# Attention on eight cores: softmax sums moved out of step with PV, and a pair's closing transposes moved into the next pair

## The reference, cut to what matters

```
x: (4, 4096, 1024), 16 heads of 64
q, k, v = x @ Wq.T, x @ Wk.T, x @ Wv.T
attn = softmax(q k^T / 8);  out = attn v
x = layernorm(x + out)
probs = softmax(x @ router_w.T + router_b); top 6 of 16, renormalised
y = sum over experts e of gate[:, e] * (x @ expert_w[e]) (+ small eps terms)
x = layernorm(x + y)
```

## Time and profile before

| | |
|---|---|
| Median of 3 runs | 2958.87 us |
| The profiled execution | 2957.79 us |
| Its span on core 2, from the first to the last instruction | 2956.3 us |
| Spans of the 8 cores | 2940.2 to 2956.3 us |
| Mean granted TensorE clock of the cores | 0.908 to 0.910 |
| TensorE, ScalarE, VectorE busy | 80%, 38%, 24% of the span |
| The chain that ended last | PE 62%, ACT 14%, DVE 9%, issue 9%, DMA 4% |

### The profile page before, as it was taken

The page is one execution under the profiler, slowest core; times in us unless marked ns, Lnnn a source line. Parts: engine busy times, 40 slices in busy tenths (PEclk is TensorE's granted clock), DMA queues, the critical chain, the costliest instruction groups (busy, mean ns, idle before and its releaser), DMA issues.

```text
span 2956.3 us, 31850 instructions; the slowest of 8 cores (2940.2 to 2956.3 us)
## 1 busy us (share of the span) xinstructions
PE 2357.0 (80%) x11919; PEld 898.2 (30%) x12032; DVE 719.1 (24%) x1555; ACT 1121.8 (38%) x1153; POOL 59.7 (2%) x80
## 2 busy tenths in 40 slices
PE   6996988889888888888888343899995343899996
PEld 2442322222222222222222111344442111344442
DVE  2332200000000000000000444233336444233336
ACT  0000288889888888888887101000000101000000
POOL 1000100000000000000000000000000000000000
PEclk9998999999999999999999676999998676899998
DMA  6745799950000000000000200222223000221221
GB/s 88 99 73 86 93 108 113 108 65 1 1 1 1 1 1 1 1 1 1 1 1 20 74 15 7 86 86 75 69 86 124 26 15 8 86 86 60 84 86 57
DMA packets 48017, 146.90 MB, mean 50 GB/s; under 512 B 2752, under 2 KB 23264, under 8 KB 46848
## 3 DMA queue, kind: packets, MB, share of 16 engines
q0 software_dynamic: 43264, 128.09, 23.7%
q1 hardware_dynamic: 4608, 16.78, 1.6%
HBM read 197.32 MB, written 41.94 MB: 81 GB/s over the span
## 4 chain that ended last, share of the span: by engine, by line
PE 62%; ACT 14%; DVE 9%; issue 9%; DMA 4%; DVEq 1%; ACTq 0%; POOL 0%; SPq 0%; POOLq 0%
PE s_PS L644 30%; PE s_PS L295 12%; ACT s_RC L358 9%; PE s_PS L315 6%; PE s_PS L225 5%; PE s_PS L327 5%; ACT s_RC L355 4%; PE s_PS L246 4%; DVE s_RC L467 2%; DMA s_RC<-xfm 1%; PE s_PS L382 1%; DMA s_RC<-xqf 1%; DMA s_RB<-ewb 1%; DVE s_RA L658 1%; DVE s_RC L474 1%
## 5 line engine op out<-in xcount | busy, mean ns | idle before, releaser
L644 PE MATMUL s_PS<-s_RB,s_QO 128*128 128x512 bf16 x4008 | 921.5, 390 | 147.5 <-DVE s_gates L600 72.7
L295 PE MATMUL s_PS<-s_QO,s_RA 64*128 64x512 bf16 x2048 | 598.8, 397 | 103.4 <-ACT s_RC L358 62.9
L355 ACT ACTIVATE s_RC<-s_PS,s_cb 128x1024 bf16<-128x1024 f32 x512 | 570.7, 1115 | 198.0 <-PE s_PS L295 184.6
L644 PEld LDWEIGHTS s_PS<-s_RB,s_QO 128*128 128x128 bf16 x4096 | 407.2, 100 | 657.8 <-issue 208.2
L358 ACT ACTIVATE s_RC<-s_PS,s_cb 128x1024 bf16<-128x1024 f32 x512 | 567.1, 1108 | 0.3
L315 PE MATMUL s_PS<-s_RC,s_RB 128*64 128x512 bf16 x2048 | 330.3, 402 | 11.4 <-ACT s_RC L358 11.4
L702 ACT ACTIVATE s_tE<-s_tB 128x1 f32<-128x1 f32 x16 | 3.2, 203 | 881.1 <-DVE s_tB L694 881.1
L327 PE MATMUL s_PS<-s_RC,s_ozb 128*64 128x512 bf16 x2048 | 319.0, 390 | 0.0
L372 DVE CAST s_QO<-s_PS 128x1024 bf16<-128x1024 f32 x16 | 19.6, 1225 | 1190.2 <-PE s_PS L327 1190.2
L295 PEld LDWEIGHTS s_PS<-s_QO,s_RA 64*128 64x128 bf16 x2048 | 118.3, 94 | 541.7 <-issue 541.7
L661 DVE SCALAR_TENSOR_TENSOR s_RB<-s_PS,s_gates,s_RA 128x1024 f32<-128x1024 f32 x128 | 164.2, 1283 | 275.3 <-PE s_PS L644 275.3
(11 more groups left out here) (76 smaller groups left out, 634.6 us busy)
## 6 DMA issues: line engine op xcount, KB each, us to landing
s_RB<-ewb POOLq DMA_DIRECT2D x32, 2048.0 KB, 9.7
ewb<-ew POOLq DMA_DIRECT2D x16, 2048.0 KB, 171.8
s_RC<-xfm POOLq DMA_DIRECT2D x16, 1024.0 KB, 11.9
s_RC<-xtm SPq DMA_DIRECT2D x16, 512.0 KB, 3.5
y<-s_RC SPq DMA_DIRECT2D x16, 512.0 KB, 2.6
s_RC<-xqf POOLq DMA_DIRECT2D x4, 1024.0 KB, 18.3
s_RC<-wkT POOLq DMA_DIRECT2D x1, 2048.0 KB, 17.7
s_QO<-wvT POOLq DMA_DIRECT2D x1, 2048.0 KB, 27.9
```

Source lines behind the costliest of these rows:

```text
L295: ins = t.matmul(PS[:, head * 1024 + qc * 512: head * 1024 + (qc + 1) * 512], RA[rows, c * SQ + kc * 128: c * SQ + (kc + 1) * 128], QO[row ...
L355: sc.activation(P[:, 0:1024], PS[:, 0:1024], AF.Exp, bias=cb3[:, :], scale=0.125).then_inc(sE, 1)
L644: ins = t.matmul(PS[:, pb + jh * 512: pb + (jh + 1) * 512], QO[:, dc * TOK + t_i * 128: dc * TOK + (t_i + 1) * 128], wbuf(par)[:, dc * 102 ...
```

## The change

The helper `emit_pvz` becomes two, `emit_pv` and `emit_z`, which are issued separately. PV(kc-1) stays behind the scores of step kc. Z does not: steps 1 to 3 of a pair issue none, step 4 issues Z(0), Z(1) and Z(2), and each step from 5 on issues Z(kc-2), behind PV(kc-1). At the end of the pair PV(31) is followed by Z(30) and Z(31). PV(0) waits for the two large copies of the pair before, Z(0) for its small copies. The exp of step kc waits for the count behind Z(kc-4).

The transposes and the small copies of a pair are issued by `emit_ftz` in step 2 of the next pair, between its scores and PV(1). Those of the last pair stand at the end of the loops. The number of matmuls, transposes and copies is unchanged.

```
+    def emit_ftz(p_prev):
+        def ftz(t, zev=fve_cnt[p_prev]):
+            t.wait_ge(vE, zev)
+            for sl in range(8):
+                ins = t.transpose(PS[:, 3072 + sl * 128: 3072 + (sl + 1) * 128],
+                                  zs[:, sl * 128:(sl + 1) * 128], idf[:, :])
+            ins.then_inc(tV, 1)
+        q("tensor", ftz)
...   (fvz: the 16 small copies, as before)
+                if kc == 2 and p > 0:
+                    emit_ftz(p - 1)
                 if kc > 0:
                     kcp = kc - 1
-                    ve_need = cvE.v if kcp == 0 else 0
+                    ve_need = fve_cnt.get(p - 1, 0) if kcp == 0 else 0
                     def ftPV(t, c=c, kcp=kcp, exp_need=exp_need, ve_need=ve_need):
                         t.wait_ge(sE, exp_need)
                         if ve_need > 0:
                             t.wait_ge(vE, ve_need)
-                        emit_pvz(t, c, kcp, kcp == 0, False).then_inc(tV, 1)
+                        emit_pv(t, c, kcp, kcp == 0, False).then_inc(tV, 1)
+                zl = []
+                if kc == 4:
+                    zl = [0, 1, 2]
+                elif kc >= 5:
+                    zl = [kc - 2]
+                if zl:
+                    ve_need = fvz_cnt.get(p - 1, 0) if zl[0] == 0 else 0
+                    def ftZ(t, c=c, zl=tuple(zl), ve_need=ve_need):
+                        if ve_need > 0:
+                            t.wait_ge(vE, ve_need)
+                        for kcp in zl:
+                            ins = emit_z(t, c, kcp, kcp == 0, False)
+                        ins.then_inc(tV, 1)
...
-                def fse(sc, s_done=s_done, pv_need=(ctV.v - 3 if kc >= 4 else 0),
-                        kc=kc):
+                def fse(sc, s_done=s_done, kc=kc,
+                        pv_need=(z_cnt.get((p, kc - 4), 0) if kc >= 4 else 0)):
...
             def ftPVl(t, c=c, exp_need=csE.v):
                 t.wait_ge(sE, exp_need)
-                emit_pvz(t, c, NKT - 1, False, True).then_inc(tV, 1)
+                emit_pv(t, c, NKT - 1, False, True).then_inc(tV, 1)
+            def ftZl(t, c=c):
+                for kcp in (NKT - 2, NKT - 1):
+                    ins = emit_z(t, c, kcp, False, kcp == NKT - 1)
+                ins.then_inc(tV, 1)
...   (fve: the two large copies, as before; ftz and fvz at this place are gone)
+    emit_ftz(2 * NPAIR - 1)
```

More of the change, by code:

```diff
@@ L275, in build, with emit_pv, emit_z, fvz @@
     ew_cast_done = NE * 16
+    fve_cnt = {}
+    fvz_cnt = {}
+    pv_cnt = {}
+    z_cnt = {}
+    def emit_pv(t, c, kcp, first, last):
+        P = pbuf(kcp % 4)
+        for head in range(2):
+            hh = 2 * c + head
+            orow = slice(head * 64, (head + 1) * 64)
+            for qc in range(2):
+                ins = t.matmul(
+                    PS[orow, 2048 + qc * 512: 2048 + (qc + 1) * 512],
+                    RB[:, kcp * D + hh * 64: kcp * D + (hh + 1) * 64],
+                    P[:, head * 1024 + qc * 512: head * 1024 + (qc + 1) * 512],
+                    start=first, stop=last, tile_position=(0, head * 64),
+                    skip_group_check=True)
+        return ins
+    def emit_z(t, c, kcp, first, last):
+        P = pbuf(kcp % 4)
+        for head in range(2):
+            orow = slice(head * 64, (head + 1) * 64)
+            for qc in range(2):
+                ins = t.matmul(
+                    PS[orow, 3072 + qc * 512: 3072 + (qc + 1) * 512],
+                    ozb[:, :],
+                    P[:, head * 1024 + qc * 512: head * 1024 + (qc + 1) * 512],
+                    start=first, stop=last, tile_position=(0, head * 64),
+                    skip_group_check=True)
+        return ins
+    def emit_ftz(p_prev):
[6 more added lines that the diff above has]
+        q("tensor", ftz)
+        ctV.v += 1
+        ztr = ctV.v
+        def fvz(v, c=p_prev % NPAIR, h=p_prev // NPAIR, ztr=ztr):
+            v.wait_ge(tV, ztr)
+            for sl in range(8):
+                tile = h * 8 + sl
+                v.tensor_copy(rzpre[:, tile * NH + 2 * c: tile * NH + 2 * c + 1],
+                              PS[:, 3072 + sl * 128: 3072 + sl * 128 + 1])
+                ins = v.tensor_copy(
+                    rzpre[:, tile * NH + 2 * c + 1: tile * NH + 2 * c + 2],
+                    PS[:, 3072 + sl * 128 + 64: 3072 + sl * 128 + 65])
+            ins.then_inc(vE, 1)
+        q("vector", fvz)
+        cvE.v += 1
+        fvz_cnt[p_prev] = cvE.v
     for h in range(2):
@@ L344, in ftPV @@
                             t.wait_ge(vE, ve_need)
-                        emit_pvz(t, c, kcp, kcp == 0, False).then_inc(tV, 1)
+                        emit_pv(t, c, kcp, kcp == 0, False).then_inc(tV, 1)
                     q("tensor", ftPV)
                     ctV.v += 1
-                def fse(sc, s_done=s_done, pv_need=(ctV.v - 3 if kc >= 4 else 0),
-                        kc=kc):
+                    pv_cnt[(p, kcp)] = ctV.v
+                zl = []
[11 more added lines that the diff above has]
+                        ins.then_inc(tV, 1)
+                    q("tensor", ftZ)
+                    ctV.v += 1
+                    for kcp in zl:
+                        z_cnt[(p, kcp)] = ctV.v
+                def fse(sc, s_done=s_done, kc=kc,
+                        pv_need=(z_cnt.get((p, kc - 4), 0) if kc >= 4 else 0)):
                     if pv_need > 0:
@@ L364, in ftPVl, with fve @@
                 t.wait_ge(sE, exp_need)
-                emit_pvz(t, c, NKT - 1, False, True).then_inc(tV, 1)
+                emit_pv(t, c, NKT - 1, False, True).then_inc(tV, 1)
             q("tensor", ftPVl)
             ctV.v += 1
-            pv_done = ctV.v
-            def fve(v, c=c, qc0=qc0, pv_done=pv_done):
-                v.wait_ge(tV, pv_done)
+            pv_cnt[(p, NKT - 1)] = ctV.v
+            def ftZl(t, c=c):
+                for kcp in (NKT - 2, NKT - 1):
+                    ins = emit_z(t, c, kcp, False, kcp == NKT - 1)
+                ins.then_inc(tV, 1)
+            q("tensor", ftZl)
+            ctV.v += 1
+            for kcp in (NKT - 2, NKT - 1):
+                z_cnt[(p, kcp)] = ctV.v
+            pvz_done = ctV.v
+            def fve(v, c=c, qc0=qc0, pvz_done=pvz_done):
+                v.wait_ge(tV, pvz_done)
                 v.tensor_copy(QO[:, c * TOK + qc0: c * TOK + qc0 + 1024],
                               PS[:, 2048:3072])
-                v.tensor_copy(zs[:, :], PS[:, 3072:4096]).then_inc(vE, 1)
+                ins = v.tensor_copy(zs[:, :], PS[:, 3072:4096])
+                ins.then_inc(vE, 1)
             q("vector", fve)
             cvE.v += 1
[L377 to L400, removed]
+            fve_cnt[p] = cvE.v
+    emit_ftz(2 * NPAIR - 1)
     p2_ve = cvE.v
```

## The result

The changed kernel is slower, by little and clearly: the ratio to the kernel before is 1.0063, with a 95% interval of 1.0053 to 1.0074, the medians of all executions 2977.2 and 2957.6 us. It was forecast at 2937, and 2909 to 2960 was the range.

The account below looks back on a forecast made before the run. Bound: an attention loop between TensorE and ScalarE that neither fills. Waits save 2.95 us a pair, clock falls take back 1.4: 15 pairs give 23 us, net 22 after the ends, so 2958.9 to 2937 us; range 2909 to 2960.

Parts of the forecast that it names:

- The boundary: Between pairs: S(0) directly behind Z(31), first exp 2.27 us after the last exp's end instead of 6.08.
- The copies: Two large vector copies at the pair's start: hidden by steps 0 and 1, with 0.9 us to spare before PV(0).
- The transposes in step 2: Transposes between S(2) and PV(1): taken as 1.00 us, exp(3) starts at 9.30, 1.0 us late.
- The burst: Three Z in step 4: exp(4) waits for Z(2) and starts at 14.1 us, 2.8 us lost.
- The sum: Whole pair at 2.4 GHz: 76.6 us instead of 79.54, 2.95 us less.
- The clock: Sparse stretches after S(0) and the burst: one fall to 1.2 GHz in four pairs of five, costing 1.4 us a pair.
- The range: Whole kernel: 2909 to 2960 us holds 8 in 10, reaching to rival B and Rival A.
- rival B: All pairs: the gain goes back through longer clock falls, 2958 us, up to 2975; chance 0.21.
- C: PV(0) to burst end, 9.0 us, runs wholly at 1.2 GHz: pair 85.6 us, kernel 3050 us; chance 0.04.
- The ends: First pair loses 0.7 us to the burst; last pair 0.4 us, an extra Z before its last copies.
- Rival A: All pairs: clock stays fast, 44 us come off, 2915 us, or 2900 with hidden transposes; chance 0.21.
- Rival D: Mid-pair steps: pace improves from 2.235 by up to 0.22 us a step, 2844 us; chance 0.04.

Follow-up runs that it names:

- a_filled: Changed kernel plus ten useless repeats of score matmuls a pair, in steps 0, 3 and 4: 2942 us, ratio to before 0.9960.
- b_filled: Kernel before plus repeats of the next pair's scores, 20 matmuls in front of the transposes and head 1 of step 0 twice more: 2920 us, ratio 0.9903.
- move_only: Kernel before with only the transposes and small copies moved, behind S(1) in the next pair's step 1, Z not held back: 2893 us, ratio 0.9796.
- dense_5: Changed kernel with next S(0) before PV(31), Z(30), Z(31), own count for one large copy, Z(0), Z(1) in step 3, then Z(k-2): 2860 us, ratio 0.9683.
- z_from_3: Changed kernel with Z(0) and Z(1) in step 3 and Z(k-2) from step 4 on, so no burst of three: 2909 us.
- fill_early: Changed kernel with only the score matmuls of head 1 of step 0 repeated twice more: 2960 us.

## Why the prediction was wrong, point by point

- *The boundary.* Right. Exp(0) 2.27 us behind the last exp, forecast 2.27; S(0) directly behind Z.
- *The copies.* Right: hidden. PV waited for the last exp alone, 10.9 us in all (the groups of instructions).
- *The transposes in step 2.* Right at the fast clock. Exp(3) came at best 9.34 us behind the last exp (9.30 forecast). Its mean over the 15 boundaries is 11.34, by the clock.
- *The burst.* Right as a wait: exp(4) at best at 14.21, forecast 14.1. Its mean is 17.1.
- *The sum.* 76.6 us at 2.4 GHz; 76.45 measured in `a_filled`, 76.71 in the changed kernel itself. Setting it against 79.54 was no fault of the sum, since the clock was taken off next, but it hid where the gain was to come from. 79.54 holds the clock losses of before. `b_filled` shows that they are some 2.8 us a pair, and that the pair of before at 2.4 GHz takes 76.7 to 77.2. The change was worth 0.3 us a pair or less by its waits; nearly all of the forecast gain rested on the clock's costing 1.4 us after.
- *The clock.* This is the step that failed, in the term "one fall a pair in four pairs of five". What I took was 0.8 falls of 3.2 to 6.8 us, 4.0 us of low time, for 1.4 us. Measured: 10.4 us of low time, for 80.55 - 76.45 = 4.1 us. The price of a low microsecond was about right (0.35 us taken, 0.39 measured); the amount was 2.6 times too small, and beyond the 7 us that the prediction named as a sign of being wrong. I had counted the two sparse stretches, but as alternatives. They add up: a fall ahead of the burst in 14 of 15 pairs, and more than one low stretch in 10 of 15. Against the kernel before, the amount is not all. Over the eight cores, by the unrounded clock, low time rose from 8.7 to 10.3 us a pair, and what it costs from 2.6 (79.44 - 76.88, the mean of the pairs of `b_filled` at 1.00) to 3.8 us (80.35 - 76.59, that of `a_filled`), so a low microsecond costs 0.30 us before and 0.36 after. About half of the added loss is the amount, the other half the dearer microsecond. A likely reason for that, which no run shows by itself, is the place: the low clock now meets the transposes in mid-stream (1.97 us) and the burst (2.78 us), for both of which ScalarE waits.
- *The range.* Its upper end was rival B, the gain given back at about 5.9 us of low time in dense work. B is what happened, and it went a little beyond the 2975 us that I gave it. The mechanism of C, half clock through transposes and burst, did occur in single pairs (the second line of the drawing, 20 us at 1.2 GHz, 83.05 us), but not in each.
- *The ends.* The first pair lost 2.8 us, and not the 0.7 taken: from its first exp to its first vector copy it takes 423.60 - 345.99 = 77.6 us, where it took 422.61 - 347.80 = 74.8. With 15 x 1.01 that makes 18.0 us from the first exp to the last first copy; the first exp is 1.8 us earlier in this trace, and 0.9 us are added behind the last copy, which gives the 17.1 between the spans.
- *Rival A* held in the changed kernel in two of the 120 pairs of the eight cores; nearly throughout it held only in other orders, `move_only` and `dense_5`, and in `b_filled`. The Trainium skill (TensorE: Matmul & The Clock Gate, Why this matters for your kernels) warns of long idle gaps; here the clock fell at 1313.9 although no rest of TensorE behind the pair's end was over 1.35 us, as the timeline above shows. The rule of the Trainium skill that transposes don't count as activity (same page, Part 4: PE-mode transpose) is not borne out by these either: eight times fewer raised the low time from 10.4 to 16.0 us, twice as many brought it to 6.0.
- *Rival D*: no. The usual pace is still 2.235 us a step.

Left open: why the first fall comes in 14 pairs of 15 in the changed kernel and in `z_from_3`, and in two of `move_only`, whose rests behind S(0) are the same 1.35 and 0.42 us. Work in steps 1 and 2 (transposes a step earlier, Z in both) sets them apart, and the two transpose runs point to it as well. But `dense_5`, whose steps 1 and 2 are no fuller, has it in 6 of 15, and `fill_early`, with repeats in the very rest behind S(0), still in 12 of 15. Transposes and Z were not tried one by one in these steps.

## What to carry to other kernels

Before a wait is priced, split a pair (or whatever repeats) into its length at the full clock and the time at the low one: here the loss at the boundary was only in part the gap that one sees, and a schedule that shortens the gap but thins out TensorE's next steps gives it all back. Holding work back to let the critical engine run ahead is dear when it makes sparse steps and then a burst: keep the amount of work of each step as even as its dependencies allow. The best boundary was none: the next pair's first matmuls issued ahead of the last ones of this pair, and a count for each thing that somebody waits for.

## What the hardware showed that I had not expected

- Useless matmuls paid: 24 a pair more in the kernel before made it 1.0% faster, ten 512-column score repeats in the changed one 1.0% as well.
- The clock fell in 14 pairs of 15 with no rest of TensorE over 1.35 us ahead of it; with the same rests and a fuller step behind them, in `move_only`, it fell in two. The low stretches last 3 to 20 us, through dense work too (TensorE busy 6.80 of 6.80 us at 911.2).
- A microsecond at 1.2 GHz costs 0.3 to 0.4 us in this loop, where ScalarE hides part of it.
